# Cross-attention and an eight-expert feed-forward on one core: routing maxima read from PSUM, a closing expert finished by row groups, a reordered end of the routing, and a new order of the first loads

## The reference

```python
x = x + xattn(layernorm(x), ctx_1024)       # 16 sequences of 100 tokens, width 256
x = x + ffn(layernorm(x))
# xattn: q, k, v projections, rope, 16 heads of 16, a query sees keys q-64..q, softmax, output projection
# ffn:
logits = xf @ router_w.T                    # 1600 tokens, 8 experts
topk_p, topk_i = top_k(softmax(logits), 2); topk_p /= topk_p.sum(-1, keepdims=True)
for e in range(8):
    mask = (topk_i == e).any(-1)
    mean_w = (topk_p * (topk_i == e)).sum() / mask.sum()
    h = silu(xf @ gate_w[e].T) * (xf @ up_w[e].T)       # 256 -> 1024
    out += mask[:, None] * (h @ down_w[e].T) * mean_w   # 1024 -> 256
```

## Time and profile before

| | |
|---|---|
| median of 3 runs | 466.39 us (465.91 to 467.24) |
| the profiled execution's own time | 467.31 us |
| its span, first to last instruction | 465.5 us |
| PE busy | 443.7 us, 95% of the span |
| DVE, ACT, POOL busy | 302.2, 281.8, 138.3 us |
| mean granted TensorE clock | 0.982 of full speed |

### The profile page before, as it was taken

One profiled execution on the slowest core, in us unless ns is written; L12 is line 12 of the kernel. 1 busy time (PEld: TensorE's weight loads), 2 busy tenths in 40 slices (PEclk: granted clock), 3 DMA queues, 4 the chain that ended last, 5 costly groups with the idle time before them and its releaser, 6 DMA issues.

```text
span 465.5 us, 8569 instructions
## 1 busy us (share of the span) xinstructions
PE 443.7 (95%) x2553; PEld 358.7 (77%) x2553; DVE 302.2 (65%) x744; ACT 281.8 (61%) x886; POOL 138.3 (30%) x172
## 2 busy tenths in 40 slices
PE   7999999999999999999999999999999999999980
PEld 4657565657566655579999999999999999999980
DVE  3766969798989878787646647467474563763320
ACT  2388778888787888356456456465554655554230
POOL 5201014453626252575014040050220500403122
PEclk9899999999999999899999999999999999999995
DMA  5640092030303032416727636465375453311102
GB/s 166 222 110 8 18 336 73 13 103 18 106 14 112 8 110 68 128 55 199 253 86 180 212 69 180 142 144 172 93 202 174 92 175 85 42 40 21 21 10 30
DMA packets 24667, 49.90 MB, mean 107 GB/s; under 512 B 5730, under 2 KB 15494, under 8 KB 24474
## 3 DMA queue, kind: packets, MB, share of 16 engines
q1 hardware_dynamic: 12858, 22.95, 16.4%
q10 hardware_dynamic: 5616, 19.40, 14.2%
q0 software_dynamic: 6144, 6.97, 8.6%
HBM read 39.16 MB, written 13.20 MB: 112 GB/s over the span
## 4 chain that ended last, share of the span: by engine, by line
PE 80%; DVE 7%; ACT 5%; issue 3%; DMA 1%; POOL 1%; SPq 0%; ACTq 0%; POOLq 0%; DVEq 0%
PE b_s L767 8%; PE b_s L771 8%; PE b_s L768 8%; PE b_small L795 7%; PE b_o L795 7%; PE b_s L490 6%; PE b_pv L513 4%; ACT probs L942 3%; PE b_proj L543 3%; PE b_pt L499 3%; PE b_pt L767 3%; PE b_pt L771 3%; PE b_pt L768 3%; PE b_proj L569 3%; PE b_s L488 3%
## 5 line engine op out<-in xcount | busy, mean ns | idle before, releaser
L942 ACT ACTIVATE probs<-b_s,negmax 100x100 f32<-100x100 f32 x256 | 85.7, 361 | 19.4 <-DVE negmax L1278 19.2
L1500 POOL DMA_INDIRECT out<-y_sb,idnow x32 | 46.8, 1462 | 153.1 <-ACT y_sb L1002 129.8
L975 ACT CAST h_hi<-h_sb 128x448 fp32r<-128x448 f32 x64 | 36.3, 567 | 85.7 <-DVE h_sb L1362 85.7
L1254 DVE TENSOR_TENSOR w_lo<-w_raw,w_hi 128x1024 fp32r<-128x1024 f32 x48 | 58.8, 1224 | 19.5 <-ACT w_hi L906 19.5
L767 PE MATMUL b_s<-x_hi,w_lo 128*128 128x448 f32 x192 | 71.1, 370 | 0.0
L771 PE MATMUL b_s<-x_lo,w_hi 128*128 128x448 f32 x192 | 69.5, 362 | 0.0
L768 PE MATMUL b_s<-x_hi,w_hi 128*128 128x448 f32 x192 | 69.3, 361 | 0.0
L1366 DVE TENSOR_TENSOR h_lo<-h_sb,h_hi 128x448 fp32r<-128x448 f32 x64 | 40.1, 626 | 40.5 <-ACT h_hi L975 40.5
L942 ACT ACTIVATION_READ_ACCUMULATOR probs<-b_s,negmax 100x1 f32 x256 | 56.9, 222 | 0.0
L490 PE MATMUL b_s<-kblk,qrot 128*100 128x400 f32 x128 | 53.6, 499 | 0.0
L906 ACT CAST w_hi<-w_raw 128x1024 fp32r<-128x1024 f32 x48 | 50.4, 1050 | 0.0
(11 more groups left out here) (201 smaller groups left out, 896.7 us busy)
## 6 DMA issues: line engine op xcount, KB each, us to landing
w_raw<-in_ffw ACTq DMA_DIRECT2D x36, 512.0 KB, 4.0
w_raw<-in_ffw SPq DMA_DIRECT2D x12, 512.0 KB, 5.5
slots<-in_padrows SPq DMA_DIRECT2D x9, 449.8 KB, 4.6
xin<-slots SPq DMA_DIRECT2D x9, 449.8 KB, 4.5
kblk<-krot SPq DMA_DIRECT2D x120, 12.5 KB, 1.8
out<-x_all SPq DMA_DIRECT2D x8, 200.0 KB
ctx_all<-in_ctxT SPq DMA_DIRECT2D x1, 1200.0 KB, 6.3
x_all<-in_x SPq DMA_DIRECT2D x1, 1200.0 KB
```

What stands on the lines that cost most here:

```text
L942: m = nc.scalar.activation(probs[:, N % 3, h, :], b_s[N % 3][0:S, h * S:(h + 1) * S], ACT.Exp, bias=negmax[:, N % 4, h:h + 1], accum_out=p ...
L1254: V.tensor_tensor(w_lo[1 - par][:, cols], w_raw[:, cols], w_hi[1 - par][:, cols], ALU.subtract).then_inc(s_wlo, 1)
L1500: G.indirect_dma_start(out, bass.IndirectOffsetOnAxis(idnow[:, n:n + 1], 0), y_sb[:, n, :], None, bounds_check=TOK + TILE - 1, oob_is_err= ...
```

## The change

The order of first loads becomes x, context, then only the first 638 columns of `cst`; the tables are rearranged so that the start's parts lie in front, and the other 376 columns follow after the router's small tables under a semaphore of their own (`s_cst2`). Idle matmuls of the start become 10, 3 and 6 instead of 8, 2 and 3. `choose` has no copy of the logits. The residual of the last pair is done per sequence (`last_residual`), and several steps around it move; the warm matmuls there change. Piece 5 of expert 0's low weights, and with it the next load of that piece, move behind the routing. The first tile's token numbers are loaded by POOL. In the last expert the down projection runs five chunks behind and ends group by group, with a signal per group and the groups alternating over two banks. Columns of `columns_down` signal by two instead of one, which changes no wait's moment.

```diff
--- before.py
+++ after.py
@@ -52,15 +52,17 @@
-C_ID, C_TRI, C_ONE, C_MASK = 0, 128, 256, 384
-C_ROPE = C_MASK + S
...
+C_ID, C_ROPE = 0, 128
+C_MASK = C_ROPE + 4 * S
+C_HEAD = C_MASK + S
+C_PAR = C_HEAD + HC
+C_TRI = C_PAR + 2
+C_ONE = C_TRI + 128
+C_EXP = C_ONE + 128
...
@@ -361,13 +365,15 @@
-            load_rows(0, 0, 1)
-            sp.dma_start(cst[:, :], consts).then_inc(s_cst, 16)
+            sp.dma_start(x_all[:, 0:2, :], x[0:2].rearrange("b s d -> s b d")).then_inc(s_x[0], 16)
+            sp.dma_start(ctx_all[:, :, 0:PT], ctxT[:, :, 0:PT]).then_inc(s_ctx[0], 16)
+            sp.dma_start(cst[:, 0:C_TRI], consts[:, 0:C_TRI]).then_inc(s_cst, 16)
             sp.wait_ge(s_cst, 16)
...
             sp.dma_start(rows_sb[:, :], rownum).then_inc(s_w, 16)
+            sp.dma_start(cst[:, C_TRI:C_ALL], consts[:, C_TRI:C_ALL]).then_inc(s_cst2, 16)
             load_rows(1, 1, 2)
@@ -408,8 +414,6 @@
-            for k in range(NPAIR - 3, WCH):
-                second_weights(k)
@@ -426,6 +430,8 @@
             write_tail(1)
+            for k in range(NPAIR - 3, WCH):
+                second_weights(k)
@@ -437,14 +443,14 @@
-            sp.dma_start(idnext[:, :].bitcast(F32),
-                         slots[0:TILE, D:RW].rearrange("(p g) w -> p (g w)", g=GRP),
-                         allow_slow_non_contiguous=True).then_inc(s_ids0, 16)
@@ -585,18 +591,20 @@
+                if r == 2 * NPAIR - 1:
+                    pe.wait_ge(s_x2a, 1)
                 for k in range(DC):
...
             def x2_transpose(i):
-                if i == NPAIR - 1:
-                    pe.wait_ge(s_xc, 1)
-                else:
+                if i < NPAIR - 1:
                     pe.wait_ge(s_xr, i + 1)
                 small_free()
                 for b in range(2):
+                    if i == NPAIR - 1:
+                        pe.wait_ge(s_xc, b + 1)
@@ -688,26 +695,28 @@
                     if n == 5 and i == NPAIR:
-                        warm(5)
-                        early_tile()
-                        warm(5)
+                        warm(8)
                         x2_transpose(NPAIR - 1)
                     if n == 5 and 0 <= i - 2 < NPAIR:
                         ranks(i - 2)
-                    if n == 2 and prv:
+                    if n == 5 and i == NPAIR:
+                        early_tile(0)
+                    if n == 2 and prv and i < NPAIR:
                         den_transpose(2 * i - 1)
...
                     if n == 0 and i == NPAIR + 1:
-                        warm(3)
+                        warm(1)
                     if n == (4 if i == 0 else 3) and nxt:
                         if i < 0:
-                            idle(2)
+                            idle(3)
                         q_project(i + 1)
                         if i < 0:
-                            idle(3)
+                            idle(6)
                     if 0 <= N - 2 < NQ * NPAIR:
                         probs_transpose(N - 2)
+                    if n == 1 and i == NPAIR:
+                        den_transpose(2 * i - 1)
...
                         if i < 0:
-                            idle(8)
+                            idle(10)
                         xn_transpose(i + 1)
...
-                    if n == 2 and i == NPAIR:
-                        warm(2)
                     if n == 2 and 0 <= i - 2 < NPAIR:
                         route_logits(i - 2)
                     if n == 2 and i == NPAIR:
+                        warm(4)
+                    if n == 2 and i == NPAIR + 1:
+                        early_tile(1)
+                        late_rows(NPAIR - 2, (0,))
                         warm(1)
-                    if n == 2 and i == NPAIR + 1:
-                        warm(3)
-                        late_rows(NPAIR - 2)
...
-            warm(5)
+            late_rows(NPAIR - 2, (1,))
+            warm(2)
             late_rows(NPAIR - 1)
@@ -777,16 +786,18 @@
                 for g in groups:
-                    o = b_y[g // 2][0:ROWS, g % 2 * D:(g % 2 + 1) * D]
+                    o = b_y[g % 2][0:ROWS, g // 2 * D:(g // 2 + 1) * D]
...
-                    if f == FC - 1 and g % 2:
+                    if f == FC - 1:
                         m.then_inc(s_down, 1)
@@ -816,28 +827,29 @@
-                    if f >= 3:
-                        (project_down if last else columns_down)(par, t, f - 3)
+                    if f >= 5 and last:
+                        project_down(par, t, f - 5)
+                    elif f >= 3 and not last:
+                        columns_down(e, par, t, f - 3)
...
-                for f in range(FC - 3, FC - 1):
-                    project_down(par, t, f, range(2))
-                project_down(par, t, FC - 1, range(2))
-                for f in range(FC - 3, FC - 1):
-                    project_down(par, t, f, range(2, GRP))
-                project_down(par, t, FC - 1, range(2, GRP))
+                for g in range(GRP):
+                    if g >= DC:
+                        pe.wait_ge(s_y, GRP * t + GRP + g - DC + 1)
+                    for f in range(FC - 5, FC):
+                        project_down(par, t, f, (g,))
...
-                pe.wait_ge(s_wlo, WCH * (e + 1))
+                pe.wait_ge(s_wlo, WCH * (e + 1) if e else WCH - 1)
@@ -923,7 +935,7 @@
-                    if n == 1 and i == NPAIR:
+                    if n == 2 and i == NPAIR:
                         rows_high(NPAIR - 2)
@@ -983,15 +995,14 @@
                 for n in range(GRP):
-                    if n % 2 == 0:
-                        a.wait_ge(s_down, 2 * t + n // 2 + 1)
-                    nc.scalar.activation(y_sb[:, n, :], b_y[n // 2][0:ROWS, n % 2 * D:(n % 2 + 1) * D],
+                    a.wait_ge(s_down, GRP * t + n + 1)
+                    nc.scalar.activation(y_sb[:, n, :], b_y[n % 2][0:ROWS, n // 2 * D:(n // 2 + 1) * D],
                                          ACT.Copy, scale=meanw[0:ROWS, e:e + 1]).then_inc(s_y, 1)
@@ -1148,11 +1160,22 @@
+            def last_residual(b):
+                i = NPAIR - 1
+                v.wait_ge(s_o, 2 * i + b + 1)
+                v.wait_ge(s_xob, i + 1)
+                xs = x_all[:, 2 * i + b, :]
+                done = s_x2 if b else s_x2a
+                V.tensor_tensor(xs, b_o[0:S, b * D:(b + 1) * D], xs, ALU.add).then_inc(done, 1)
+                v.wait_ge(done, i + 1 if b else 1)
+                link(V.bn_stats(stats2[:, b, :], xs))
+                ins = V.bn_aggr(mv2[:, b, :], stats2[:, b, :])
...
+                V.tensor_scalar(xn[:, b, :], xs, mv2[:, b, 0:1], None, ALU.subtract).then_inc(s_xc, 1)
@@ -1166,15 +1189,14 @@
             def choose(i):
                 v.wait_ge(s_lg, i + 1)
-                V.tensor_copy(logits[:, :, :].rearrange("p b e -> p (b e)"), b_small[0:S, 0:2 * E]).then_inc(s_lgc, 1)
-                v.wait_ge(s_lgc, i + 1)
                 for b in range(2):
-                    V.max(top[:, i, b, :], logits[:, b, :]).then_inc(dve, 1)
+                    V.max(top[:, i, b, :], b_small[0:S, b * E:(b + 1) * E]).then_inc(dve, 1)
                     links[0] += 1
                 v.wait_ge(dve, links[0])
                 for b in range(2):
-                    V.max_index(topi[:, b, :], top[:, i, b, :], logits[:, b, :]).then_inc(dve, 1)
-                    links[0] += 1
+                    ins = V.max_index(topi[:, b, :], top[:, i, b, :], b_small[0:S, b * E:(b + 1) * E])
+                ins.then_inc(s_lgc, 1)
+                v.wait_ge(s_lgc, i + 1)
@@ -1287,10 +1309,10 @@
-                    if n == 1 and 0 <= i - 3 < WCH:
+                    if n == 1 and 0 <= i - 3 < WCH - 1:
                         weights_low(-1, 1, i - 3)
                     if n == 1 and i == NPAIR:
-                        rows_low(NPAIR - 2)
+                        last_residual(0)
@@ -1304,14 +1326,15 @@
                     if n == 3 and i == NPAIR:
-                        residual(i - 1)
-                        rows_center(i - 1)
+                        last_residual(1)
...
+                    if n == 3 and i == NPAIR:
+                        rows_low(NPAIR - 2)
@@ -1323,7 +1346,7 @@
-                    if n == 6 and prv:
+                    if n == (7 if i == NPAIR - 1 else 6) and prv:
                         rows_write(i - 1)
@@ -1396,6 +1419,7 @@
             V.tensor_tensor(meanw[:, :], b_o[:, 0:E], crec[:, :], ALU.mult).then_inc(s_mean, 1)
+            weights_low(-1, 1, WCH - 1)
@@ -1478,6 +1502,12 @@
             scatter(NPAIR - 1)
+            for q in s_scat:
+                g.wait_ge(q, 16 * TOPK * 2 * (NPAIR // 2))
+            g.wait_ge(s_tails[0], 16)
+            G.dma_start(idnext[:, :].bitcast(F32),
+                        slots[0:TILE, D:RW].rearrange("(p g) w -> p (g w)", g=GRP),
+                        allow_slow_non_contiguous=True).then_inc(s_ids0, 16)
```

64 lines of the change are left out of this document (34 added, 30 removed).

## The result

The changed kernel takes 461.10 us (median of 15 runs, 460.49 to 465.52), the kernel before on the same chip 466.32 (15 runs, 465.91 to 467.50). The ratio is 0.9903, 95% interval 0.9886 to 0.9920: 4.5 us less, between 3.7 and 5.3. The forecast was 460.1, in a range of 458.1 to 463.2. The sign and the range hold; the sum was 1.1 us too large by the medians (6.3 against 5.2). Of its four terms the last tile's was right. The start's was right in size, but mostly by another cause. The maxima came to nothing. The end of the attention shows in the traces at full clock, but not in the time of the runs with that part alone.

A forecast was written before the change was run, and what follows sets the result against it. PE, busy 95% of the span, was taken as the bound. Terms 3.2 + 1.0 + 1.2 + 0.9 = 6.3 us off the profiled 467.3 gave 461.0, and 460.1 as median; range 458.1 to 463.2.

The forecast's parts named there:

- last tile: Last expert's close: groups complete one by one, POOL's adds stay 1.77 apart and start earlier; 3.2 us less.
- The start: First loads and projections: no PE gap, so the clock stays and the query projection takes 1.37; 1.2 us less.
- The maxima: Routing in the attention: maxima read from PSUM without the logits copy, 5 pairs x 0.20; 1.0 us less.
- The end of the attention: Last pair's residual, logits copy and reordered steps on DVE, ACT and PE; 0.9 us less.
- Rival 3: Reading PSUM is slow for maxima, 0.065 us more per operation: 461.6; chance 0.1.
- Rival 1: Clock falls in PE's gap before the key projection, so the start gains nothing: 462.9; chance 0.2.
- (a): End of the attention: only half the residual remains behind the last output projection, 1.1 instead of 1.79; 0.7 less.
- (c): End of the attention: first residual half fills DVE's wait, denominators' copy freed, but `rows_write` comes later; 0.1 less together.
- (d): End of the attention: pair 6's `rows_low`, 0.69, lies between centring and late one-hot matrices on DVE; 0.13 more.
- (b): End of the attention: the last pair's logits copy is gone; 0.2 less.
- Rival 2: Output projection at the attention's end runs at 2.4 GHz, another 1.0 less: 459.1; chance 0.15.
- The token numbers: First tile's load through POOL, counted at nothing: `idnow` written 5.0 us before DVE needs it.

The follow-up runs named there:

- e3_start: Kernel before with only the new order of first loads, split constants and idle matmuls 10, 3, 6: 465.80 us, ratio 0.9976.
- e2_maxima: Kernel before with only the router's maxima read from PSUM, without the logits copy: 466.99 us, ratio 1.0004.
- f1_copy_back: Changed kernel with the copy of the logits put back: 464.88 us.
- e4_end: Changed kernel with the old start, logits copy and close, leaving the attention's end, weight pieces and token numbers new: 466.57 us, ratio 0.9996.
- f3_fewer_idle: Changed kernel with 4 instead of 10 idle matmuls ahead of the first transposes: 461.02 us.
- f4_more_fill: Changed kernel with four more fillers on PE at the end of the attention: 460.82 us.
- g1_both: Changed kernel with 4 instead of 10 idle matmuls in the start and four more fillers at the attention's end: 460.49 us.
- f2_early_tile: Kernel before with the early tile's transposes moved on PE behind the last x2 transposes and ranks, five fillers less: 472.89 us, ratio 1.0028.
- e1_close: Kernel before with only the last expert's new close, five chunks group by group: 463.19 us, ratio 0.9922.
- g3_ids_pool: Kernel before with only the first token numbers loaded on POOL's queue instead of SP's: 470.07 us, ratio 1.0033.
- g4_pieces: Kernel before with last weight pieces issued behind the early tile's load and piece 5's low part made after routing: 466.60 us, ratio 0.9971.

## Why the prediction was right or wrong

- **The last tile, 3.2 less: right.** The adds 1.78 apart, the fourth 1.5 behind PE, and 3.6 (2.8 to 4.5) alone. The reason was right as well: with three chunks POOL binds again.
- **The maxima from PSUM, 1.0 less: wrong, it is nothing.** The step that failed is "5 pairs x 0.20", which took a stretch of the chain for time that can be had. I gave the other end, "only turns into a wait for PE", as a bound, and it was the case: 0.18 of the 0.20 shows as that wait. The chain of waits names one path; that PE had no gap beside it for over 7 us was in the same trace, and should have decided. Rival 3's mechanism is refuted, at 0.001 and 0.007 us per operation.
- **The start, 1.2 less: the size right, the mechanism for the most part not, so luck.** Alone it gives 1.1. The clock did stay where the profile of before had lost it. But I took that loss as the rule and took it off the median, and five of the seven traces with the old start keep the full clock. The step that failed is "That alone is worth nothing", of the earlier x. I gave transposes that come sooner only as a bound, and they are 0.8 of the gain; the clock is about 0.3. The context lands at 6.1 to 6.9 and not near 7.2 (the key projection starts at 6.14 in the changed kernel, at 6.89 in `e3_start`), and the transposes no longer wait for x. Rival 1 didn't come.
- **The end of the attention, 0.9 less: not seen in the median, 0.2 less alone (1.1 less to 0.8 more); at full clock 1.6.** The working of (a) was right: from the addition to the centring it is 1.14 instead of 1.80 (`e2_maxima`), 0.7 less. For (c) I had 0.1, and the addition itself starts 0.4 sooner. Together they bring the centring 1.05 sooner. What I missed is that PE stood behind the early tile's rows, which cost 0.6 behind the centring and is gone. Without it, and with the low part of (d) added, the stretch from the centring to the first product is 9.20 instead of 9.79; the copy of (b) is gone in both. So at full clock it is 188.67 - 187.03 = 1.6. In the one trace of this part alone the same stretch takes 11.38, with the granted clock at 0.50 for most of it. Whether the clock also holds its median run back isn't shown. Rival 2 came in the profile but was worth little: with the old end at full clock (`e2_maxima`) PE only waited longer for the rows, 188.67 against 189.09 from the scores to the first product, 0.4 and not 1.0.
- **What no rival had:** a slow clock in the late rows, in a fifth of the runs, for 4 us. That is read from the traces of `f1_copy_back` and `e4_end` and the spread of the changed kernel's times. I gave the fillers "24 to 16" a sentence and costed it at nothing. The runs speak for the fillers as what keeps the clock where DVE is late, without proving it.
- **The sum.** By the parts measured alone the terms were 3.6 for 3.2, nothing for 1.0, 1.1 for 1.2 and 0.2 for 0.9: the maxima and the end fell short by 1.7 to 1.9, and the close gave 0.4 more. Each of these has an interval of about 0.6 to 1 us to either side. That the forecast came within 1 us of the median is in part such errors setting each other off.
- **The token numbers, costed at nothing: hidden in the changed kernel's trace.** `idnow` is written by 223.86 and DVE needs it at 227.07, 3.2 us of cover where it was 5.0. Alone, on the third chip, the edit took 1.5 more (0.1 to 2.9), which no trace explains:

```profile
223.65 0.21 POOL L1524 COPY idnow<-idnext 112x4 int32<-112x4 int32 x1 [4.08 <-issue]
```

```profile
227.07 0.16 DVE L1379 COPY idnext<-xin 112x4 int32<-112x4 int32 x1
```

PE's last product ended at 447.60, where I had written 448.4.

## What to carry to other kernels

Before a stretch of the chain is counted as gain, look at the engine that it hands over to: if that has no gap beside it, the stretch is a near tie and shortening it buys a wait. A stretch that costs something in one profile may cost nothing in most executions, so look at several before it is taken off the median. In an engine's fixed order, work whose data comes by DMA belongs behind work that is ready; a slow clock in a single profile can hide such a wait. And fillers removed from a waiting TensorE may not be free: judge them over many runs, by the spread and not the median alone.

## What the runs showed that I hadn't expected

**The gain depends on the chip.** The kernel before took 466.6, 471.8 and 467.8 us on the three chips of the experiments; `f3_fewer_idle` and `f4_more_fill` took 461.0 and 460.8 on the second, `g1_both` 460.5 on the third, no more than the changed kernel's 461.1. So beside the kernel before the gain is 11 us on the second chip and 7 on the third, where the variants' own edits are worth some tenths. Two descendants of the kernel before show a stall in the first tile there. ACT in `f2_early_tile`; on the first chip (`e1_close`, `e2_maxima`) ACT is idle for 1.6 between the first two, waiting for DVE, and the last comes at once behind the cast of the weights between them:

```profile
206.22 0.55 ACT L971 ACTIVATE act<-b_s 128x448 f32<-128x448 f32 x1
209.48 0.57 ACT L975 CAST h_hi<-h_sb 128x448 fp32r<-128x448 f32 x1 [2.71 <-issue]
...
214.58 0.54 ACT L971 ACTIVATE act<-b_s 128x448 f32<-128x448 f32 x1 [3.58 <-remote]
```

ACT waits 2.71 us for nothing that the profile shows and then 3.58; DVE and PE follow it, PE for 3.64, and the clock falls behind that. `g3_ids_pool` has the same with 2.28, and PE waits 1.98. The descendants of the changed kernel on these two chips show it weaker or hardly at all. Ahead of that cast, where the traces of the first chip have 1.3 to 1.8 spent on waiting for DVE, ACT is idle for 2.47 in `f4_more_fill` and at most 1.8 in the others; ahead of an activation it waits up to 2.01 in `f1_copy_back` and 1.58 in `f3_fewer_idle`. PE never waits more than 0.74 in any of them. `g4_pieces` shows none, and neither does the profile of the changed kernel, which was taken where the kernel before takes 466.3. What the stall is, which edit keeps it from PE, and how much of the 11 and 7 us it makes up, stays open: no experiment took the kernel before itself under the profiler on these two chips.
